# Token mixer's table in HBM: reads of 128 rows for 125, eight bank buffers for four, another order of the groups, two PSUM banks for the last quarter

## What is computed

```python
# x (64, 125, 128); Wl (124, 128); Wc (512, 128, 31); W2 (128, 512)
logits = (x @ Wl.T + bl).reshape(B, T, 4, 31)            # 31 taps around each position, masked at the ends
w = softmax(logits, -1)
y = einsum('bthk,btkhd->bthd', w, neighbours of x) + bias  # dynamic convolution over time
z = conv1d(y, Wc, 'VALID') + bc                          # 128 -> 512 channels, 31 taps, 125 -> 95 positions
h = selu(z) @ W2.T + b2
```

## Time and profile before

| what | value |
|---|---|
| median of 3 runs | 2176.36 us (2175.88, 2176.36, 2190.74) |
| profiled execution, its own time | 2189.58 us |
| its span, first to last instruction | 2187.6 us |
| outside the span | 2.0 us |
| mean granted TensorE clock | 0.937 |
| PE busy over the span | 1915.4 us (88%) |
| DVE, ACT, POOL busy | 1527.8, 1231.8, 964.8 us |

### The profile page before, as it was taken

How to read it: one execution, slowest core, us unless ns; L and a number is a source line. 1 busy time by engine, 2 the same in 40 slices (tenths; PEclk the granted TensorE clock), 3 DMA queues, 4 the chain that set the end, 5 groups by cost and what they waited for, 6 DMA issues and landing times. The chain is left out here.

```text
span 2187.6 us, 46198 instructions
## 1 busy us (share of the span) xinstructions
PE 1915.4 (88%) x16314; PEld 1322.7 (60%) x16314; DVE 1527.8 (70%) x3461; ACT 1231.8 (56%) x2203; POOL 964.8 (44%) x870
## 2 busy tenths in 40 slices
PE   5888999979997999999999997998888888677772
PEld 4678887745554566666666664666665566446552
DVE  4533445558886999999999985777776666655655
ACT  2443345445553777677776775776665566325552
POOL 0000000024553988888888883014434433635552
PEclk9998999989999999999999999999999889688996
DMA  7964443379910000000000001000000000246665
GB/s 276 330 243 144 142 154 135 117 278 412 413 73 11 11 10 10 10 10 10 10 10 10 10 10 29 2 2 12 12 12 14 19 11 11 64 146 165 167 169 191
DMA packets 128783, 211.27 MB, mean 97 GB/s; under 512 B 27316, under 2 KB 96613, under 8 KB 119245
## 3 DMA queue, kind: packets, MB, share of 16 engines
q1 hardware_dynamic: 120044, 192.88, 26.3%
q0 software_dynamic: 6624, 12.70, 1.7%
q10 hardware_dynamic: 1920, 3.11, 0.4%
HBM read 98.38 MB, written 111.25 MB: 96 GB/s over the span
## 5 line engine op out<-in xcount | busy, mean ns | idle before, releaser
L1262 POOL TENSOR_TENSOR b_pool_c<-b_pool_b 128x512 f32<-128x512 f32 x384 | 492.3, 1290 | 109.8 <-ACT b_pool_b L1189 61.6
L1189 ACT ACTIVATE b_pool_b<-b_pool_a,c_b 128x1024 f32<-128x1024 f32 x384 | 436.6, 1150 | 176.6 <-DVE b_pool_a L1425 160.9
L1425 DVE TENSOR_TENSOR b_pool_a<-b_p_s,c_shares 128x1024 f32<-128x1024 f32 x384 | 454.2, 1214 | 52.5 <-PE b_p_s L1028 45.2
L1026 PE MATMUL b_p_s<-c_x_hi,c_w_hi 128*128 128x512 f32 x384 | 295.1, 769 | 5.1 <-DVE b_pool_a L1425 5.1
L1033 PE MATMUL b_p_y<-b_pool_c,c_w 128*128 128x512 f32 x384 | 195.8, 591 | 0.0
L1033 PE MATMUL b_p_p<-b_pool_c,c_w 128*128 128x512 f32 x384 | 194.8, 591 | 0.0
L1203 POOL MEMSET b_ln_power<- 96x4 f32 x1 | 0.1, 98 | 440.2 <-POOLq L67 440.2
L689 POOL TENSOR_TENSOR d_ln_rstd<-d_ln_var,d_ln_power 128x2 f32<-128x2 f32 x48 | 33.9, 706 | 316.4 <-DVE d_ln_var L685 316.4
L2678 POOL DMA_INDIRECT e_again<-e_by,e_xb x111 | 109.2, 984 | 110.8 <-ACT e_by L2655 71.3
L1027 PE MATMUL b_p_s<-c_x_lo,c_w_hi 128*128 128x512 f32 x384 | 153.2, 399 | 0.0
L1314 DVE TENSOR_TENSOR b_pool_b<-b_p_s,b_decay 96x384 f32<-96x384 f32 x256 | 124.6, 546 | 39.8 <-PE b_p_s L897 39.5
(11 more groups left out here) (349 smaller groups left out, 4621.0 us busy)
## 6 DMA issues: line engine op xcount, KB each, us to landing
slots<-b_pool_c SPq DMA_DIRECT2D x55, 1040.0 KB, 25.1
e_wb<-e_weights SPq DMA_DIRECT2D x111, 164.0 KB
band_scratch<-a_work SPq DMA_DIRECT2D x16, 1024.0 KB, 5.5
a_work<-band_scratch SPq DMA_DIRECT2D x16, 1023.5 KB, 7.8
a_work<-z_scratch SPq DMA_DIRECT2D x64, 250.0 KB
z_scratch<-a_work SPq DMA_DIRECT2D x56, 256.0 KB, 2.7
a_raw<-in_Wc SPq DMA_DIRECT2D x16, 512.0 KB, 8.3
e_xb<-slots SPq DMA_DIRECT2D x111, 65.0 KB
```

The source lines that it names most:

```text
L1026: nc.tensor.matmul(p_h[q % SLOTS][:, 0:WIDE], w1_hi[:, q, :], x_hi[s][:, :], start=True, stop=False)
L1189: nc.scalar.activation(hid[q % SLOTS][:, :, :], gelu_in[q % SLOTS][:, :, :], ACT.Gelu, bias=b1[:, q:q + 1]).then_inc(s_ge, 1)
L1262: nc.gpsimd.tensor_tensor(both[q % SLOTS][:, :], hid[q % SLOTS][:, 0, :], hid[q % SLOTS][:, 1, :], ALU.add).then_inc(s_bo, 1)
L1425: v.tensor_tensor(gelu_in[q % SLOTS][:, :, :], p_h[q % SLOTS][:, 0:WIDE].unsqueeze(1).to_broadcast([128, 2, WIDE]), shares[s][:, :, :], AL ...
```

## The change

The table gets 128 rows, and reads take all of them. The three rows that no product fills are filled once with zeros from a new input. The bank buffers are eight, the counts `EARLY` are 6, 4 and 4 by quarter, and 4 groups are held back at the end in every quarter. Groups 48 to 63 go to `p_A[0]` and `p_A[1]` by turns.

```diff
-        ZW, ZR = 4, 8
-        EARLY, LATE_OF_LAST = 6, 4
+        ZW, ZR = 8, 8
+        EARLY, HELD = (6, 4, 4), 4
...
-        zt = [carve(NF2, GB, 128) for s in range(ZR)]
+        zt = [carve(128, GB, 128) for s in range(ZR)]
...
-        spectra = [nc.dram_tensor(f"z_scratch{s}", (NF2, NB, 128), F32, kind="Internal").ap() for s in range(2)]
+        spectra = [nc.dram_tensor(f"z_scratch{s}", (128, NB, 128), F32, kind="Internal").ap() for s in range(2)]
+
+        def conv(k):
+            return p_A[k % 2] if k >= NG * (NO - 1) else p_y
...
         def beside_bank(o, i):
-            k = NG * (o - 1) + EARLY + i // 2
-            return k if o > 0 and i % 2 == 1 and not (o == NO - 1 and i // 2 >= NG - EARLY - LATE_OF_LAST) else None
+            if o == 0 or i % 2 == 0 or EARLY[o - 1] + i // 2 >= NG - HELD:
+                return None
+            return NG * (o - 1) + EARLY[o - 1] + i // 2
 
         def beside_weights(o, late):
-            k = NG * o + late - (CHUNK - EARLY)
+            k = NG * o + late - (CHUNK - EARLY[o])
             return k if k >= 0 else None
...
+            for padded in spectra:
+                sp.dma_start(padded[NF2:128, :, :], w["none"]).then_inc(s_pad, 16)
+            sp.wait_ge(s_pad, 16 * 2)
             for i in range(4, 7):
                 load_raw(i)
             for o in range(NO):
                 for i in range(NBK):
                     write_z(o, i)
-                    if o > 0 and i in (1, 3):
-                        read_z(NG * (o - 1) + EARLY + ZR + i // 2)
+                    k = beside_bank(o, i)
+                    if k is not None and k + ZR < NG * o:
+                        read_z(k + ZR)
+                for g in range(ZR if o == 0 else ZR - HELD):
+                    read_z(NG * o + g)
                 if o < NO - 1:
-                    load_raw(4 * o + 7)
-                    for g in range(ZR):
-                        read_z(NG * o + g)
-                    for g in range(EARLY):
-                        if o < NO - 2 and g % 2 == 1:
-                            load_raw(4 * o + 8 + g // 2)
-                        read_z(NG * o + ZR + g)
-            for g in range(NG):
-                read_z(NG * (NO - 1) + g)
+                    for late in range(CHUNK):
+                        if late % 2 == 1 and 4 * o + 7 + late // 2 < NO * MPO // MPC:
+                            load_raw(4 * o + 7 + late // 2)
+                        if beside_weights(o, late) is not None:
+                            read_z(beside_weights(o, late) + ZR)
+            for k in range(NG * (NO - 1) + ZR - HELD, NG * NO):
+                read_z(k)
...
             def to_time(k):
                 pe.wait_ge(s_zr[k % ZR], 16 * (k // ZR + 1))
-                if k >= 1:
+                if k >= NG * (NO - 1):
+                    pe.wait_ge(s_zs[k % 2], NBK // 2 * NO)
+                    pe.wait_ge(s_zc, k - 1)
+                elif k >= 1:
                     pe.wait_ge(s_zc, k)
                 for n in range(GB):
-                    last = nc.tensor.matmul(p_conv[:, n * SP:(n + 1) * SP], zt[k % ZR][:, n, :], idft[:, :],
+                    last = nc.tensor.matmul(conv(k)[:, n * SP:(n + 1) * SP], zt[k % ZR][0:NF2, n, :], idft[:, :],
                                             start=True, stop=True, skip_group_check=True)
...
-            for k in range(NG * (NO - 1) - LATE_OF_LAST, NG * NO):
+            for k in range(NG * (NO - 1) - HELD, NG * NO):
                 group(k)
...
+    d["none"] = np.zeros((128 - NF2, NB, 128), np.float32)
```

More of the change, by code:

```diff
@@ L137, in phase_token_mixer @@
         p_y = pb("p_y")
-        p_conv, p_out = p_y, p_log
+        p_out = p_log
         s_first, s_dft, s_late = sem("const_first"), sem("const_dft"), sem("const_late")
@@ L150, in phase_token_mixer @@
         s_zmm, s_zs = sem("z_product"), [sem("z_copied_act"), sem("z_copied_dve")]
+        s_pad = sem("table_padded")
         s_zw, s_zr = [sem(f"z_written{s}") for s in range(ZW)], [sem(f"z_read{s}") for s in range(ZR)]
@@ L484, in exp_z @@
                     act.wait_ge(s_rz, k - 1)
-                nc.scalar.activation(zc[g % 2], p_conv[:, 0:N].rearrange("o (n s) -> o n s", n=GB), ACT.Identity,
+                nc.scalar.activation(zc[g % 2], conv(k)[:, 0:N].rearrange("o (n s) -> o n s", n=GB), ACT.Identity,
                                      bias=vecs(o)).then_inc(s_zc, 1)
```

## The result

The changed kernel takes 2151.58 us, median of 4 runs (2147.34 to 2155.61), beside 2181.91 us of the kernel before in 4 (2175.88 to 2190.74). The ratio is 0.9865, with a 95% interval of 0.9835 to 0.9896: faster by 1.35%, between 1.0 and 1.7%. The forecast was 27.8 us and a time of 2148.6 us, inside 2142 to 2165. The profiled execution takes 2154.22 us with a span of 2151.3 us.

The account below looks back on a forecast made before the run. Slow table reads, 2.1 us each on 5 of 16 engines, were taken to set the mixer's waits. Terms of 11.9 + 4.3 + 4.4 + 7.2 = 27.8 us off the 2176.4 us median gave 2148.6 us, range 2142 to 2165.

Parts of the forecast that it names:

- Reads of 128 rows: Table reads in the token mixer: spread over 16 engines, each takes 0.7 us of the engines instead of 2.1.
- Weight stretches of quarters 1 and 2: Second and third weight stretches: older groups first hide the late read, 22.7 us each, gain 11.9 us (10 to 12).
- Weight stretch after quarter 0: First weight stretch: a read pause goes and the clock returns sooner, gain 4.3 us (1.2 to 6).
- The pause of 2.87 us: First weight stretch: TensorE's wait for its first table read goes, counted as 2.9 us.
- The 1.4 us for the clock: First weight stretch: less time at the low clock once the read pause is gone, 1.4 us.
- Banks and buffers: Bank stretches of quarters 1 and 2: waits for writes go, 40.5 us each, gain 4.4 us (3.5 to 4.5).
- The end: Last 20 groups: from group 48 on 1.65 us a group, gain 7.2 us (4.1 to 8.9).
- the second rival: Last groups: the chain over ACT and DVE keeps 1.87 us a group; gain 24.7 us, 2151.7 us, chance 0.10.
- What is added: End of the band stage: two 96 KB transfers and SP's wait, 3 engines at most, 30 us cover, cost 0.
- The first: Table reads stay at 2.1 us, older groups and buffers still gain: 17.8 us, 2158.6 us, chance 0.06.
- The third: Behind the mixer or in the runs' state, part is given back: gain 13.8 us, 2162.6 us, chance 0.17.
- The fourth: Quarter 1's banks and following weights: clock stays low, 35.4 us slower, 2211.8 us, chance 0.04.

Follow-up runs that it names:

- the repeat: The changed kernel itself, with no further edit, measured again beside the kernel before: 2165.3 us beside 2191.4, ratio 0.9870.

## Why the prediction was right, point by point

**What bounds the kernel.** The reads of 125 rows on 5 engines were the cause of most waits. Shown: the rows taken back lose 15.9 us of measure (271.5 for 255.6), the rows alone gain 16.7, and either figure is more than half of the 27.6.

**Reads of 128 rows.** Held. The estimate was 0.7 us a read at 388 GB/s; the burst of reads ran at 344 GB/s, which is 0.76. No group waits, 126 rows do the same, and 127 take 10.6 us.

**Weight stretches of quarters 1 and 2.** The size held, 11.8 us for 11.9. The prediction gave all of it to the new order, and it is shared: wide reads alone bring 8.0 of it (24.9 and 24.5 us), the order alone 9.9 (24.8 and 22.7), and both together 11.8, since they remove the same pauses.

**Weight stretch after quarter 0.** 4.2 us for 4.3, but partly by luck. The pause of 2.87 us is gone in every run with the new order and fast reads. The order alone removes it too (that run's first group starts at 196.09 without idle time), and the wide reads alone leave 1.04 of it. The 1.4 us for the clock is not a fixed gain: the same code of this stretch took 24.2, 25.5 (four buffers), 26.7 (one bank), 27.3 (the repeat) and 28.8 us (all held in two banks), with mean clocks of 0.86 in the first, 0.75 and 0.70 in the last two. The kernel before had 28.4, and 27.3 and 28.5 with unrelated edits. The clock falls near 195 us, behind the two pauses for DVE's copies and in every run, as the prediction said (that they cause it was not tested); when the clock comes back differs from run to run, and so the gain here is between nothing and 4 us. The bounds of 1.2 to 6 were too high at the lower end.

**Banks and buffers.** 4.3 us for 4.4, and "either edit alone would remove it" is shown from both sides. The new order alone removes 3.4 of it, which the prediction did not see. That SP's queue was full of reads is read from the issue times, 3.29 us for a write and 0.47 with fast reads.

**The end.** 7.3 us for 7.2, at 1.63 us a group for 1.65. From the first matmul of group 44 to the last projection the reads alone give 3.8 (2.08 to 1.87 a group) and the bank another 3.8 (1.87 to 1.63), the bank only behind the reads; some 0.2 goes to a later start of group 44, which now follows a group. The low bound of 4.1 at 1.87 us a group, which the second rival uses too, is 3.9 by the prediction's own numbers (438.58 - 406.6 - 15 x 1.87).

**What is added.** Free, as said: the zeros had landed at 151.6 us. That they go over 3 engines at most was wrong: each of the two is 16 packets of 6 KB with 16 small ones, so 16 engines, and lands in 2.7 us. Each is one unbroken piece of 96 KB at both ends; whether that is the reason was not tested. The longer line of reads before the load of raw weights is free only with fast reads. That was not said in the prediction.

**The rivals.** The first, slow reads with the rest kept, was priced at a gain of 17.8 us. It was built, and gains 11.7, of which 1.6 are the banks of quarter 0. The step that failed is "the stretch after quarter 0 would gain some 1.5": it loses 5.9, by the late load of raw weights. The same lateness (1.71 us at 280.17) leaves 10.1 for the 11.9 of the other two, and the end gains 1.7 for 0. The second, 1.87 us in spite of two banks, is refuted by the 1.63. The third had an upper level of the runs in it; the kernel before was measured twice at 2187 to 2191 us and twice at 2176, and the four runs of the changed one lie within 8.3 us of each other, so the gain was seen whole, but by how the runs fell and not by an argument. The fourth did not come in the changed kernel. A small form of it was seen with two banks in the kernel before: a pause for a write of 2.86 us inside the banks of quarter 2, the clock low, and that stretch at 45.1 us for 42.9.

**Sum.** 27.8 us forecast, 27.6 in the mixer of the profiled pair, 25.6 in the repeat. That the first two agree to 0.2 is partly luck, by the clock of the first weight stretch. The medians differ by 30.3 us, and by 26.1 in the repeat. The median of the kernel before lies between its two levels; from the 2176.36 that the prediction started from, it is 24.8.

## What to carry to other kernels

Look at the DMA share when one kind of transfer runs alone: a flat share of 5/16 is a sign that a transfer uses few engines, and padding its outermost dimension by three rows can be worth more than a reordering (here 16.7 us for 9.4). Then ask of every edit what it is worth once the largest one is in: here the buffers fall to nothing, the second PSUM bank rises from nothing to 3.8 us, and the new order, which costs 5.7 us in one place with slow reads, becomes harmless. When a transfer is moved behind others in one queue, price it by the time these take to be issued, and say under which speed of theirs the price is zero.

## What was not expected

One row fewer than 128 makes a read of this table fifteen times slower than the estimate for 128: 10.6 us for 0.7. A queue full of transfers on five engines holds back the others too: the bank write, which has 128 partitions, took 3.29 us to issue behind them and 0.47 without. And the same instructions of the first weight stretch differ by 4.6 us between runs (24.2 to 28.8) with the mean granted clock (0.86 to 0.70). In the longest, TensorE stood idle nowhere from 193.2 us on, and its chunks still took 2.08 us each until 208.5.
